# Second graph attention: where the VectorE passes over a score tile read and write

## The chip, the cores and the metric

The kernel runs on one core of one Trainium2 chip. The metric is the device time in microseconds of one execution; the figures given for a kernel are the median and the lowest and highest of its runs. TensorE is called PE here, VectorE DVE, ScalarE ACT, GpSimd POOL and SyncE SP, as in the profile.

## The reference

The program is two graph attentions over 12,500 nodes and 200,000 edges sorted by target node, each followed by a residual and a layer norm. The change touches the second one alone:

```python
src = concatenate([edge_index[0], loops]); dst = concatenate([edge_index[1], loops])
xp = (x @ W).reshape(n, H, C)                       # 12500 x 4 heads x 64
a_src = einsum('nhc,hc->nh', xp, att_src)
a_dst = einsum('nhc,hc->nh', xp, att_dst)
alpha = leaky_relu(a_src[src] + a_dst[dst], negative_slope=0.2)
amax = segment_max(alpha, dst)
ex = exp(alpha - amax[dst])
w = ex / segment_sum(ex, dst)[dst]
agg = segment_sum(xp[src] * w[..., None], dst)
out = elu(agg.reshape(n, H * C) + bias)
```

The result is added to x and normed. The self loops (`loops`) are handled by the kernel apart, block by block.

## The kernel before

The stage is `attend_plain`; its tiles' names begin with `plain_` in the trace. The edges are cut into 521 tiles of 384 (`MAIN`), each with 32 spill-over slots taken from the next tile, so that a tile has 416 slots (`SLOTS`) on the free axis. The 128 partitions are 4 heads by 32 target nodes (`TN`).

For tile t the engines do this, each in its own queue:

- POOL (`gather`, L1286) issues three indirect DMAs of 128 rows each from `xp` into `rows`, a ring of 8 tiles. Before tile t it waits only for `agg_done` of tile t-8, the tile that last used the slot.
- SP (`fetch`, L1307) loads `a_dst`, one value per partition, into a ring of 4, and puts results away (`put_out`, L1326, for tile t-7, stands just ahead of it). It also loads masks and indices.
- PE (`score`, L1378) transposes the source scores of the gathered rows into PSUM `p_s` (two buffers), [128 x 416].
- ACT (`move`, L1540) adds `a_dst` as a bias and copies `p_s` to SBUF `alpha`. ACT (`set_apart`, L1531) makes `far` in bf16: zero where slot and target node belong together and immense elsewhere.
- DVE (`lower_bound`) subtracts `far` from `alpha` and takes the maximum along the row (L1424, a fused pass and a read of its accumulator into `raw`), applies the leaky factor to the maximum (L1428, one column) and to the whole tile (L1429, 416 columns), and makes two one-column values from the maximum (L1433 `LOW`, L1434 `KEEP`). Both L1424 and L1429 read two SBUF operands of full width.
- ACT (`weigh`, L1548) takes the exponential. PE (`turn_weights`, L1363, L1364) transposes the weights into PSUM `p_w`, DVE (`copy_weights`, L1417) copies them to SBUF, PE (`aggregate`, L1391) sums the messages in `p_o` with 16 matmuls, and ACT (`put`, L1556, L1559) copies them out.

Once for each of 98 blocks of 128 nodes, DVE, ACT and SP also join the sums, add the self loop, and norm (`join`, `weigh_parts`, `gather_parts`, `finish`, `end_norm`): L1440, L1473, L1479, L1483 and L1486 are DVE passes of 256 or 264 columns with two SBUF operands.

The order in each queue is written out: `interleave` walks the steps n, and a `TilePart(lag, fn)` does tile n - lag in step n. On DVE step n holds `copy_weights` of tile n-3, `lower_bound` of tile n-1, then block work. On ACT it holds `move` of n-1, `set_apart` of n, `put` of n-4, block work, `weigh` of n-1. On PE it holds `turn_weights` of n-3, `score` of n-1, `aggregate` of n-4. Sixteen steps have three blocks' work among them. The first attention, `attend_typed`, is built alike, but its DVE pass L989 reads the scores straight from PSUM, `typed_p_s`, and its gathers are L765.

Of the kernel before, what the change touches and what calls it, by code (L numbers as in the profile page):

```python
# [10 lines left out]
ALU = mybir.AluOpType  # L11
ACT = mybir.ActivationFunctionType
AX = mybir.AxisListType.X

P = 128
# [19 lines left out]
SLOTS = MAIN + SPILL  # L35
# [1174 lines left out]
def attend_plain(k):  # L1210
# [3 lines left out]
    R, M, SCORE, TURN_LAG, LAG = 8, 4, 1, 3, 4  # L1214
    LOADS = 16
    FIRST = 73
    HALF = PERIOD // 2
    A_SRC, A_DST = VW, VW + P
    with Stage(nc, "plain") as z:
# [3 lines left out]
        far = z.sb("far", [P, 2, SLOTS], BF16)  # L1223
        a_dst = z.sb("a_dst", [P, M, 1])
        alpha = z.sb("alpha", [P, 2, SLOTS])
        raw = z.sb("raw", [P, 2])
        weight = z.sb("weight", [P, 2, SLOTS])
        weight_t = z.sb("weight_t", [P, 2, 4 * P])
        col = z.sb("col", [P, 4, 3])
        MAXED, LOW, KEEP = range(3)  # L1230
        result = z.sb("result", [P, 4, AG])
        one = z.sb("one", [P, 1])
        agg = z.sb("agg", [P, 2, HEADS * AG])
# [23 lines left out]
        p_s = z.ps("p_s", [P, 2, 512])  # L1257
# [1 line left out]
        p_o = z.ps("p_o", [P, 2, 512])  # L1259
        rows_in, match_in, index_in, result_out, slab_in = z.sems("rows_in", R), z.sems("match_in", M), z.sems("index_in", 4), z.sems("result_out", 4), z.sems("slab_in", 2)  # L1260
        own_in, out_ = z.sems("own_in", GROUP), z.sems("out", GROUP)
        (settled, slot_free, setup, init_done, far_ready, scores_ready, max_ready, low_ready, raw_ready, moved, alpha_ready, exp_done, turned,
         weight_t_ready, agg_done, result_ready, later_in) = (z.sem(n) for n in (
            "settled", "slot_free", "setup", "init_done", "far_ready", "scores_ready", "max_ready", "low_ready", "raw_ready", "moved", "alpha_ready",
            "exp_done", "turned", "weight_t_ready", "agg_done", "result_ready", "later_in"))
        settled4, keep_ready = z.sem("settled4"), z.sem("keep_ready")
        (agg_in, joined, self_added, self_ready, empty_ready, top_ready, peak_ready, below_ready, scaled_ready, weighed, total_ready, whole_ready,
# [24 lines left out]
        @block.sync  # L1292
        def _(sp):
            places = [sp.alloc_register(f"sp_place{j}") for j in range(TPB)]
            put_places = [sp.alloc_register(f"sp_put1_{j}") for j in range(TPB)]

            def fetch_index(g, at):
                sp.dma_start(index[:, g], k.idx[:, at]).then_inc(index_in[g], 16)

            def fetch(t):  # L1300
                m = t.slot(M)
                node = first_nodes(k, sp, t, places)
                if not t.known_below(M):
                    sp.wait_ge(moved, t.n - M + 1)
                    sp.sem_inc(slot_free, 1)
                with nc.allow_non_contiguous_dma(reason="one value per node and head"):
                    sp.dma_start(a_dst[:, m], k.xp[bass.ds(node, TN), A_DST:V1].rearrange("n (h o) -> h n o", o=1)).then_inc(match_in[m], 16)  # L1307
                if t.slot(TPB) == 2 and not (isinstance(t.q, int) and t.n + 2 >= TILES):
                    g, group = group_of(t)
                    if not t.known_below(TPB):  # L1310
                        sp.wait_ge(far_ready, t.n - 2)
                        sp.sem_inc(slot_free, 1)
                    fetch_slab((g + 1) % 2, bass.ds(t.n + 2, TPB))
                if t.slot(TPB) == TPB - 1:
                    g, group = group_of(t)
                    fetch_index((g + EARLY) % 4, bass.ds((group + EARLY) * CALLS, CALLS))

            def fetch_slab(slot, at):
                sp.dma_start(match[:, slot], k.match[1, at].unsqueeze(0).broadcast_to((P, TPB, SLOTS))).then_inc(slab_in[slot], 16)

            def put_out(t):
                m = t.slot(4)
                node = first_nodes(k, sp, t, put_places)
                sp.wait_ge(result_ready, t.n + 1)
                sp.sem_inc(slot_free, 1)
                sp.dma_start(k.agg[t.slot(2), bass.ds(node, TN)].rearrange("n h c -> h n c"), result[:, m]).then_inc(result_out[m], 16)  # L1326

            def load(b):
                o = b.slot(GROUP)
                if not b.known_below(GROUP):  # L1330
                    sp.wait_ge(self_done, b.n - GROUP + 1)
                sp.dma_start(own[:, o], k.xp[bass.ds(b.n * P, P), :]).then_inc(own_in[o], 16)
                sums_settled(sp, b, result_out, slot_free)
                if not b.known_below(1):
                    sp.wait_ge(joined, b.n)
                sp.dma_start(agg[:], k.agg[:, bass.ds(b.n * P, P)].rearrange("a n h c -> n a (h c)")).then_inc(agg_in, 16)

            def store(b):
                o = b.slot(GROUP)
                sp.wait_ge(res_ready, b.n + 1)  # L1340
                sp.dma_start(k.out[bass.ds(b.n * P, P), :], res[:, o]).then_inc(out_[o], 16)

            for g in range(EARLY):
                fetch_index(g, slice(g * CALLS, g * CALLS + CALLS))
            fetch_slab(0, slice(0, TPB))
            sp.wait_ge(setup, 1)
            interleave(sp, FIRST, TilePart(7, put_out), TilePart(0, fetch), BlockPart(1, 3, store), BlockPart(0, 0, load))
            for j in range(4):
                sp.wait_ge(result_out[j], 16 * -(-(TILES - j) // 4))
            groups = TILES // TPB + EARLY  # L1350
            for g in range(4):
                sp.wait_ge(index_in[g], 16 * -(-(groups - g) // 4))
            for o in range(GROUP):
                sp.wait_ge(out_[o], 16 * -(-(ROWS - o) // GROUP))

        @block.tensor
        def _(pe):
# [8 lines left out]
            def score(t):  # L1366
                c, r = t.slot(2), t.slot(R)
                if not t.known_below(2):
                    pe.wait_ge(moved, t.n - 1)
                pe.wait_ge(rows_in[r], t.use(R) * (16 * CH) + 16 * CH)  # L1370
                for j in range(CH + 1):
                    e = P if j < CH else SPILL
# [39 lines left out]
        def _(v):  # L1412
            def copy_weights(t):
# [2 lines left out]
                    v.wait_ge(agg_done, t.n - 1)  # L1416
                v.tensor_copy(weight_t[:, t.slot(2)], p_w[:, t.slot(2)]).then_inc(weight_t_ready, 1)  # L1417

            def lower_bound(t):
                c, m = t.slot(2), t.slot(4)  # L1420
                v.wait_ge(moved, t.n + 1)
                v.wait_ge(far_ready, t.n + 1)
                v.sem_inc(settled4, 1)
                v.tensor_tensor_reduce(alpha[:, c], alpha[:, c], far[:, c], 1.0, -3.0e38, ALU.subtract, ALU.max,  # L1424
                                       accum_out=raw[:, c:c + 1]).then_inc(raw_ready, 1)
                v.wait_ge(raw_ready, t.n + 1)
                maxed = col[:, m, MAXED:MAXED + 1]
                v.scalar_tensor_tensor(maxed, raw[:, c:c + 1], 0.2, raw[:, c:c + 1], ALU.mult, ALU.max).then_inc(max_ready, 1)  # L1428
                v.scalar_tensor_tensor(alpha[:, c], alpha[:, c], 0.2, alpha[:, c], ALU.mult, ALU.max).then_inc(alpha_ready, 1)  # L1429
                v.wait_ge(max_ready, t.n + 1)  # L1430
                if not t.known_below(4):
                    v.wait_ge(result_ready, t.n - 3)
                v.tensor_scalar(col[:, m, LOW:LOW + 1], maxed, NOEDGE, -1.0, ALU.max, ALU.mult).then_inc(low_ready, 1)  # L1433
                v.scalar_tensor_tensor(col[:, m, KEEP:KEEP + 1], maxed, NOEDGE, maxed, ALU.is_gt, ALU.mult).then_inc(keep_ready, 1)  # L1434

# [78 lines left out]
            for to in (p_w, result):  # L1514
# [1 line left out]
            init(v.memset(one[:], 1.0))  # L1516
            v.wait_ge(init_done, count)
            v.sem_inc(setup, 1)
            interleave(v, FIRST, TilePart(TURN_LAG, copy_weights), TilePart(SCORE, lower_bound),
                       BlockPart(2, 0, join), BlockPart(3, 1, gather_parts), BlockPart(4, 0, weigh_parts),  # L1520
                       BlockPart(5, 1, finish), BlockPart(6, 1, end_norm))

# [1 line left out]
        def _(act):  # L1524
# [6 lines left out]
                act.activation(far[:, t.slot(2)], match[:, slab, t.slot(TPB)], ACT.Square, bias=cst[:, C_CODE:C_CODE + 1],  # L1531
                               scale=FAR).then_inc(far_ready, 1)

            def move(t):
                c, m = t.slot(2), t.slot(M)
                act.wait_ge(match_in[m], t.use(M) * LOADS + LOADS)
                act.wait_ge(scores_ready, t.n + 1)
                if not t.known_below(2):
                    act.wait_ge(exp_done, t.n - 1)
                act.activation(alpha[:, c], p_s[:, c, 0:SLOTS], ACT.Identity, bias=a_dst[:, m]).then_inc(moved, 1)  # L1540

            def weigh(t):
                c = t.slot(2)
                if not t.known_below(2):
                    act.wait_ge(turned, t.n - 1)
                act.wait_ge(low_ready, t.n + 1)
                act.wait_ge(alpha_ready, t.n + 1)
                act.activation(weight[:, c], alpha[:, c], ACT.Exp, bias=col[:, t.slot(4), LOW:LOW + 1]).then_inc(exp_done, 1)  # L1548

            def put(t):  # L1550
# [26 lines left out]
            def grow(b):  # L1577
                act.wait_ge(h_ready, b.n + 1)
                if not b.known_below(1):
                    act.wait_ge(y_ready, b.n)  # L1580
                act.activation(grown[:], h[:], ACT.Exp, bias=one[:, 0:1]).then_inc(grown_ready, 1)

            act.wait_ge(setup, 1)
            interleave(act, FIRST, TilePart(SCORE, move), TilePart(0, set_apart), TilePart(LAG, put),
                       BlockPart(3, 0, scale), BlockPart(4, 1, grow), BlockPart(5, 0, own_parts), TilePart(SCORE, weigh))


# [1343 lines left out]
```

## Time and profile before

| | us |
|---|---|
| median of 3 runs | 4631.05 |
| lowest, highest | 4630.45, 4632.06 |
| span of the profiled execution | 4627.2 |
| gathers of the first attention | 350.6 to 2454.5 |
| gathers of the second attention | 2533.2 to 4569.1 |
| from the last gather to the end | 58.1 |

The page gives PE 85% of the span, DVE 74%, POOL 68% and ACT 60%. These are means over stages that have different limits, so the stage of the second attention is read by itself. A POOL instruction of kind DMA_INDIRECT is the issue of one gather, and its duration is the time POOL was occupied with issuing, not the time of the transfer. An idle time "<-issue" is one in which the engine waited for nothing that the profile shows.

### The profile page before, as it was taken

What the parts mean: (1) busy time and instruction counts of PE and PEld (TensorE: products, weight loads), DVE (VectorE), ACT (ScalarE), POOL (GpSimd) and SP (SyncE); (2) the same over time, 40 slices, a digit from 0 to 9 for tenths busy, and PEclk for the clock granted to TensorE, in tenths of its full rate; (3) what the DMA queues carried; (4) which work ended last, traced back from release to release, by engine and by line L of the source; (5) the groups of instructions that cost most, each with busy time, mean ns of one, the idle gap of its engine ahead of it and who ended that gap; (6) DMA issues with size and microseconds to landing.
All of it is one profiled execution on the core that took longest, in us unless ns stands there. A gap on an engine that the chain in (4) does not pass through costs nothing. (4 is left out here: it accounts for less than half of the span.)

```text
span 4627.2 us, 149696 instructions
## 1 busy us (share of the span) xinstructions
PE 3929.3 (85%) x42462; PEld 2568.6 (56%) x42462; DVE 3415.2 (74%) x11602; ACT 2795.2 (60%) x7985; POOL 3143.2 (68%) x3229
## 2 busy tenths in 40 slices
PE   6988999999999999999996778778877877777874
PEld 4655555555555555555554556555555555555553
DVE  3235788777777778777775578888778778787777
ACT  2324555555555555555553677777777777777775
POOL 1217777777777777777772777777777777777773
PEclk9998999999999999999997677777778777787777
DMA  6878888888888888888884777777777777777774
GB/s 207 282 236 246 259 259 259 257 259 259 259 255 260 258 260 258 257 258 261 259 256 120 187 206 206 207 204 205 207 207 205 205 204 205 205 208 209 203 206 131
DMA packets 820558, 1052.06 MB, mean 227 GB/s; under 512 B 458633, under 2 KB 632338, under 8 KB 820464
## 3 DMA queue, kind: packets, MB, share of 16 engines
q0 software_dynamic: 225072, 726.83, 53.9%
q1 hardware_dynamic: 594078, 323.35, 27.0%
q10 hardware_dynamic: 1314, 0.99, 0.1%
q14 instruction: 80, 0.66, 0.0%
q8 instruction: 14, 0.23, 0.0%
HBM read 915.79 MB, written 133.39 MB: 227 GB/s over the span
## 5 line engine op out<-in xcount | busy, mean ns | idle before, releaser
L1286 POOL DMA_INDIRECT plain_rows<-xp,plain_index x1563 | 1559.8, 998 | 554.9 <-issue 440.8
L765 POOL DMA_INDIRECT typed_rows<-kv,typed_index x1563 | 1511.2, 967 | 626.2 <-issue 414.3
L1391 PE MATMUL plain_p_o<-plain_rows,plain_weight_t 128*64 128x130 f32 (+1 forms) x8336 | 856.5, 348 | 44.0 <-DVE plain_weight_t L1417 43.3
L1158 ACT ACTIVATE typed_weight<-typed_weight,typed_col 128x416 f32<-128x416 f32 x521 | 334.6, 642 | 855.0 <-DVE typed_col L991 809.5
L1378 PE MATMUL plain_p_s<-all_cst,plain_rows 128*128 128x128 f32 (+1 forms) x2084 | 455.0, 318 | 368.2 <-DMA plain_rows<-xp,plain_index 365.9
L1391 PEld LDWEIGHTS plain_p_o<-plain_rows,plain_weight_t 128*64 128x64 f32 (+1 forms) x8336 | 570.2, 169 | 203.8 <-issue 128.5
L1378 PEld LDWEIGHTS plain_p_s<-all_cst,plain_rows 128*128 128x128 f32 (+1 forms) x2084 | 335.2, 174 | 522.6 <-issue 504.8
L989 DVE CUSTOM_DVE_ANT_0 typed_weight<-typed_p_s,typed_far 128x416 f32<-128x416 f32 x521 | 305.1, 586 | 371.5 <-PE typed_p_s L874 347.8
L874 PE MATMUL typed_p_s<-typed_kt,typed_q 64*32 64x416 f32 x4168 | 472.4, 521 | 103.4 <-issue 73.0
L1424 DVE CUSTOM_DVE_ANT_0 plain_alpha<-plain_alpha,plain_far 128x416 f32<-128x416 f32 x521 | 310.0, 595 | 311.4 <-ACT plain_alpha L1540 296.4
L962 DVE TENSOR_TENSOR typed_kt<-typed_p_kt,typed_rel 128x768 f32<-128x768 f32 x521 | 494.7, 950 | 3.7 <-PE typed_p_kt L851 3.4
L1548 ACT ACTIVATE plain_weight<-plain_alpha,plain_col 128x416 f32<-128x416 f32 x521 | 331.4, 636 | 256.2 <-DVE plain_col L1433 250.4
L851 PE MATMUL typed_p_kt<-all_cst,typed_rows 128*128 128x128 f32 x3126 | 458.4, 283 | 6.8 <-DMA typed_rows<-kv,typed_index 6.3
L1559 ACT COPY plain_result<-plain_p_o 32x65 f32<-32x65 f32 x2084 | 425.4, 204 | 18.2
L889 PE MATMUL typed_p_o<-typed_rows,typed_weight_t 128*32 128x65 f32 (+1 forms) x16672 | 413.4, 225 | 3.0 <-ACT typed_result L1165 0.4
L1363 PE MATMUL plain_p_w<-all_cst,plain_weight 128*128 128x128 f32 x1563 | 360.5, 351 | 50.0 <-ACT plain_weight L1548 48.9
L851 PEld LDWEIGHTS typed_p_kt<-all_cst,typed_rows 128*128 128x128 f32 x3126 | 334.6, 142 | 98.2 <-issue 90.6
L1540 ACT ACTIVATE plain_alpha<-plain_p_s,plain_a_dst 128x416 f32<-128x416 f32 x521 | 316.7, 608 | 119.9 <-PE plain_p_s L1378 95.7
L1417 DVE COPY plain_weight_t<-plain_p_w 128x512 f32<-128x512 f32 x521 | 355.3, 682 | 32.1 <-PE plain_p_w L1364 20.5
L889 PEld LDWEIGHTS typed_p_o<-typed_rows,typed_weight_t 128*32 128x32 f32 (+1 forms) x16672 | 279.6, 108 | 168.2 <-issue 91.1
L1531 ACT ACTIVATE plain_far<-plain_match,all_cst 128x416 bf16<-128x416 uint8 x521 | 328.6, 631 | 9.0 <-DMA plain_match<-match 9.0
L1138 ACT ACTIVATE typed_far<-typed_match,all_cst 128x416 bf16<-128x416 uint8 x521 | 334.0, 641 | 0.0
(190 smaller groups left out, 6303.5 us busy)
## 6 DMA issues: line engine op xcount, KB each, us to landing
typed_match<-match SPq DMA_DIRECT2D x131, 208.0 KB
plain_match<-match SPq DMA_DIRECT2D x131, 208.0 KB
agg<-qkv_zero SPq DMA_DIRECT2D x98, 264.0 KB
typed_agg<-agg SPq DMA_DIRECT2D x98, 264.0 KB
plain_agg<-agg SPq DMA_DIRECT2D x98, 264.0 KB
kv<-qkv_kv SPq DMA_DIRECT2D x98, 258.0 KB
typed_kinds<-match SPq DMA_DIRECT2D x131, 192.0 KB
typed_rows<-kv,typed_index POOLq DMA_INDIRECT x1563
```

The lines of the kernel that those rows point to most:

```text
L765: pool.indirect_dma_start(rows[:, r, j, :], None, k.kv, bass.IndirectOffsetOnAxis(ap=index[:, g, at:at + 1], axis=0)).then_inc(rows_in[r], 16)
L851: last = pe.transpose(p_kt[:, pair, j * P:j * P + P], rows[:, t.slot(R), j, pair * P:pair * P + P], ident)
L874: last = pe.matmul(p_s[at:at + TN, 0:SLOTS], q[own, m, :, h // 2], kt[own, h // 2, lo:lo + SLOTS], start=True, stop=True, tile_position=(H ...
L889: last = pe.matmul(p_o[at:at + TN, 0:V], weight_t[0:e, t.slot(2), j * P + at:j * P + at + TN], v[:, D + V * h:D + V * h + V], start=j == 0 ...
L962: v.tensor_tensor(kt[:, :, lo:lo + MAIN], p_kt[:, :, 0:MAIN], both_pairs(0, MAIN), ALU.add).then_inc(kt_ready, 1)
L1158: act.activation(weight[:, c], weight[:, c], ACT.Exp, bias=col[:, t.slot(4), LOW:LOW + 1]).then_inc(exp_done, 1)
L1286: pool.indirect_dma_start(rows[:, r, j, :], None, k.xp, bass.IndirectOffsetOnAxis(ap=index[:, g, at:at + 1], axis=0)).then_inc(rows_in[r], 16)
L1363: pe.transpose(p_w[:, t.slot(2), j * P:j * P + P], weight[:, t.slot(2), j * P:j * P + P], ident)
L1378: last = pe.transpose(p_s[:, c, j * P:j * P + e], a_src[:, A_SRC:A_DST], ident[0:e, 0:e])
L1391: last = pe.matmul(p_o[at:at + HC, t.slot(2), 0:2 * V], weight_t[0:e, t.slot(2), j * P + at:j * P + at + HC], val[:, 2 * V * g:2 * V * g + ...
L1417: v.tensor_copy(weight_t[:, t.slot(2)], p_w[:, t.slot(2)]).then_inc(weight_t_ready, 1)
L1559: last = act.copy(result[at:at + TN, m, 0:V], p_o[at:at + TN, t.slot(2), V * (h % 2):V * (h % 2) + V])
```

## The change

The leaky ReLU is made from two branches. ACT (`dampen`) writes 0.2 * score + 0.2 * a_dst into a new SBUF tile `damped`, instead of score + a_dst into `alpha`. It needs 0.2 * a_dst, which a new one-column DVE step `dampen_target` makes for tile n in step n. DVE then computes max(score + a_dst, damped) in place in PSUM `p_s`, and the pass with the maximum reads `p_s` and `far` and writes `alpha`. The maximum now is already that of the leaky scores, so L1428 and L1429 are gone. `p_s` is given back to PE at `raw_ready` instead of `moved`, and the slot of `a_dst` to SP at `leaked`.

```diff
@@ fetch (SP)
-                    sp.wait_ge(moved, t.n - M + 1)
+                    sp.wait_ge(leaked, t.n - M + 1)
@@ score (PE)
-                    pe.wait_ge(moved, t.n - 1)
+                    pe.wait_ge(raw_ready, t.n - 1)
@@ (DVE)
+            def dampen_target(t):
+                m = t.slot(M)
+                v.wait_ge(match_in[m], t.use(M) * LOADS + LOADS)
+                if not t.known_below(M):
+                    v.wait_ge(damped_ready, t.n - M + 1)
+                v.tensor_scalar(a_fifth[:, m], a_dst[:, m], 0.2, None, ALU.mult).then_inc(fifth_ready, 1)
+
             def lower_bound(t):
                 c, m = t.slot(2), t.slot(4)
-                v.wait_ge(moved, t.n + 1)
+                v.wait_ge(damped_ready, t.n + 1)
+                v.scalar_tensor_tensor(p_s[:, c, 0:SLOTS], p_s[:, c, 0:SLOTS], a_dst[:, m], damped[:, c], ALU.add, ALU.max).then_inc(leaked, 1)
                 v.wait_ge(far_ready, t.n + 1)
+                v.wait_ge(leaked, t.n + 1)
+                if not t.known_below(2):
+                    v.wait_ge(exp_done, t.n - 1)
                 v.sem_inc(settled4, 1)
-                v.tensor_tensor_reduce(alpha[:, c], alpha[:, c], far[:, c], 1.0, -3.0e38, ALU.subtract, ALU.max,
+                v.tensor_tensor_reduce(alpha[:, c], p_s[:, c, 0:SLOTS], far[:, c], 1.0, -3.0e38, ALU.subtract, ALU.max,
                                        accum_out=raw[:, c:c + 1]).then_inc(raw_ready, 1)
                 v.wait_ge(raw_ready, t.n + 1)
-                maxed = col[:, m, MAXED:MAXED + 1]
-                v.scalar_tensor_tensor(maxed, raw[:, c:c + 1], 0.2, raw[:, c:c + 1], ALU.mult, ALU.max).then_inc(max_ready, 1)
-                v.scalar_tensor_tensor(alpha[:, c], alpha[:, c], 0.2, alpha[:, c], ALU.mult, ALU.max).then_inc(alpha_ready, 1)
-                v.wait_ge(max_ready, t.n + 1)
...
+                maxed = raw[:, c:c + 1]
@@
-            interleave(v, FIRST, TilePart(TURN_LAG, copy_weights), TilePart(SCORE, lower_bound),
+            interleave(v, FIRST, TilePart(TURN_LAG, copy_weights), TilePart(SCORE, lower_bound), TilePart(0, dampen_target),
@@ (ACT)
-            def move(t):
+            def dampen(t):
                 c, m = t.slot(2), t.slot(M)
-                act.wait_ge(match_in[m], t.use(M) * LOADS + LOADS)
+                act.wait_ge(fifth_ready, t.n + 1)
                 act.wait_ge(scores_ready, t.n + 1)
                 if not t.known_below(2):
-                    act.wait_ge(exp_done, t.n - 1)
-                act.activation(alpha[:, c], p_s[:, c, 0:SLOTS], ACT.Identity, bias=a_dst[:, m]).then_inc(moved, 1)
+                    act.wait_ge(leaked, t.n - 1)
+                act.activation(damped[:, c], p_s[:, c, 0:SLOTS], ACT.Identity, bias=a_fifth[:, m], scale=0.2).then_inc(damped_ready, 1)
@@ weigh (ACT)
-                act.wait_ge(alpha_ready, t.n + 1)
```

On DVE, one step of the loop of `attend_plain` before (ISA is the fused pass with its maximum and the read of the accumulator; REGISTER_ALU is the sequencer's):

```order
L1417 COPY plain_weight_t<-plain_p_w 128x512
L1421 REGISTER_ALU
L1424 ISA plain_alpha,plain_raw<-plain_alpha,plain_far 128x416
L1424 ISA plain_raw 128x1
L1428 SCALAR_TENSOR_TENSOR plain_col<-plain_raw 128x1
L1429 SCALAR_TENSOR_TENSOR plain_alpha<-plain_alpha 128x416
L1433 TENSOR_SCALAR plain_col<-plain_col 128x1
```

And the same step of DVE's queue in the changed kernel, with its own line numbers:

```order
L1419 COPY plain_weight_t<-plain_p_w 128x512
L1430 REGISTER_ALU
L1431 SCALAR_TENSOR_TENSOR plain_p_s<-plain_p_s,plain_a_dst,plain_damped 128x416
L1437 ISA plain_alpha,plain_raw<-plain_p_s,plain_far 128x416
L1437 ISA plain_raw 128x1
L1443 TENSOR_SCALAR plain_col<-plain_raw 128x1
L1444 SCALAR_TENSOR_TENSOR plain_col<-plain_raw 128x1
```

The full-width leaky pass moved from behind the maximum to ahead of it. The one-column L1428 is gone, and L1426 (`plain_a_fifth<-plain_a_dst`) stands behind L1444 in every step, ahead of the block work. On ACT the order is the same in both kernels; its first pass of a step has another output and bias.

## Rows read from the trace of the kernel before

**Rows 1.** The page's first line.
```profile
span 4627.2 us, 149696 instructions
```

**Rows 2.** Stages by window: start:end, us, busy us and instructions per engine, clock, DMA.
```profile
core 0: us, PE busy (x) PEld busy (x) DVE busy (x) ACT busy (x) POOL busy (x), PEclk, DMA share, GB/s
350.60:2454.50 2103.90, 1990.89 (x28122) 1193.42 (x28121) 1623.71 (x4550) 1139.36 (x2835) 1511.21 (x1563) 0.99 0.89 258
...
2533.20:4569.10 2035.90, 1587.38 (x12396) 1147.83 (x12396) 1592.30 (x6404) 1507.38 (x4689) 1559.76 (x1563) 0.76 0.78 205
```

**Rows 3.** POOL's groups: busy us, mean ns | idle before and releasers; durations min/median/max.
```profile
L1286 POOL DMA_INDIRECT plain_rows<-xp,plain_index x1563 | 1559.8, 998 | 554.9 <-issue 440.8 <-DMA plain_index<-all_idx 78.7 <-PE plain_p_o L1391 35.4
L765 POOL DMA_INDIRECT typed_rows<-kv,typed_index x1563 | 1511.2, 967 | 626.2 <-issue 414.3 <-PE typed_p_o L889 178.3 <-DVEq L1125 33.6
...
L1286 POOL DMA_INDIRECT plain_rows<-xp,plain_index x1563: 942/949/1372, 2533.2 to 4568.1; - x196
```

**Rows 4.** Timeline, second attention: gathers that start inside a DVE pass (start, us).
```profile
3814.34 0.58 DVE L1429 SCALAR_TENSOR_TENSOR plain_alpha<-plain_alpha 128x416 f32<-128x416 f32 x1
3814.40 1.35 POOL L1286 DMA_INDIRECT plain_rows<-xp,plain_index  x1 [0.30 <-issue]
...
4094.78 0.59 DVE L1424 CUSTOM_DVE_ANT_0 plain_alpha<-plain_alpha,plain_far 128x416 f32<-128x416 f32 x1 [0.28 <-ACT plain_alpha L1540]
4094.95 1.24 POOL L1286 DMA_INDIRECT plain_rows<-xp,plain_index  x1 [0.30 <-PE plain_p_o L1391]
...
2964.34 0.42 DVE L1479 TENSOR_TENSOR plain_h<-plain_part,plain_self_part 128x256 f32<-128x256 f32 x1
2964.39 1.19 POOL L1286 DMA_INDIRECT plain_rows<-xp,plain_index  x1 [0.30 <-issue]
...
3800.02 0.67 DVE L1417 COPY plain_weight_t<-plain_p_w 128x512 f32<-128x512 f32 x1
3800.27 0.94 POOL L1286 DMA_INDIRECT plain_rows<-xp,plain_index  x1 [0.30 <-PE plain_p_o L1391]
```

**Rows 5.** Timeline, first attention: a gather that starts inside the pass L989.
```profile
375.76 0.59 DVE L989 CUSTOM_DVE_ANT_0 typed_weight<-typed_p_s,typed_far 128x416 f32<-128x416 f32 x1 [1.24 <-PE typed_p_s L874]
375.83 0.95 POOL L765 DMA_INDIRECT typed_rows<-kv,typed_index  x1 [0.30 <-issue]
```

**Rows 6.** DVE's groups by form, whole span.
```profile
L989 DVE CUSTOM_DVE_ANT_0 typed_weight<-typed_p_s,typed_far 128x416 f32<-128x416 f32 x521 | 305.1, 586 | 371.5 <-PE typed_p_s L874 347.8 <-DVE typed_rstd L348 11.8 <-issue 10.3
L1424 DVE CUSTOM_DVE_ANT_0 plain_alpha<-plain_alpha,plain_far 128x416 f32<-128x416 f32 x521 | 310.0, 595 | 311.4 <-ACT plain_alpha L1540 296.4 <-issue 7.1
L1429 DVE SCALAR_TENSOR_TENSOR plain_alpha<-plain_alpha 128x416 f32<-128x416 f32 x521 | 307.4, 590 | 0.0
L1433 DVE TENSOR_SCALAR plain_col<-plain_col 128x1 f32<-128x1 f32 x521 | 75.4, 145 | 0.0
L1479 DVE TENSOR_TENSOR plain_h<-plain_part,plain_self_part 128x256 f32<-128x256 f32 x98 | 41.7, 425 | 3.4
L1417 DVE COPY plain_weight_t<-plain_p_w 128x512 f32<-128x512 f32 x521 | 355.3, 682 | 32.1 <-PE plain_p_w L1364 20.5 <-issue 9.3 <-PE plain_p_o L1391 0.4
L1515 DVE MEMSET plain_p_w<- 128x1024 f32 x1 | 0.9, 912 | 11.4 <-PEq L232 11.4
```

**Rows 7.** DVE's own timeline around one tile, with ACT's L1548 behind it.
```profile
3500.49 0.59 DVE L1424 CUSTOM_DVE_ANT_0 plain_alpha<-plain_alpha,plain_far 128x416 f32<-128x416 f32 x1 [0.91 <-ACT plain_alpha L1540]
...
3501.01 0.08 DVE L1424 DVE_READ_ACCUMULATOR2_ANT plain_raw<- 128x1 f32 x1
3501.13 0.16 DVE L1428 SCALAR_TENSOR_TENSOR plain_col<-plain_raw 128x1 f32<-128x1 f32 x1
...
3501.70 0.14 DVE L1433 TENSOR_SCALAR plain_col<-plain_col 128x1 f32<-128x1 f32 x1
```

**Rows 8.** Waits from 2700 to 4400 us: us in total, times, longest.
```profile
DVE plain_alpha L1424 <- ACT plain_alpha L1540: 216.1, 275, 2.9
...
DVE plain_weight_t L1417 <- PE plain_p_w L1364: 9.9, 17, 0.9
```

**Rows 9.** SP's queue in the timeline: a result put away, then the next `a_dst` issued.
```profile
3501.88 0.61 SPq L1326 DMA_DIRECT2D agg<-plain_result  x1
...
3503.70 0.61 SPq L1307 DMA_DIRECT2D plain_a_dst<-xp  x1
```

More of the change, by code:

```diff
@@ L1225, in attend_plain @@
         alpha = z.sb("alpha", [P, 2, SLOTS])
+        a_fifth = z.sb("a_fifth", [P, M, 1])
+        damped = z.sb("damped", [P, 2, SLOTS])
         raw = z.sb("raw", [P, 2])
@@ L1228, in attend_plain @@
         weight_t = z.sb("weight_t", [P, 2, 4 * P])
-        col = z.sb("col", [P, 4, 3])
-        MAXED, LOW, KEEP = range(3)
+        col = z.sb("col", [P, 4, 2])
+        LOW, KEEP = range(2)
         result = z.sb("result", [P, 4, AG])
@@ L1261, in attend_plain @@
         own_in, out_ = z.sems("own_in", GROUP), z.sems("out", GROUP)
-        (settled, slot_free, setup, init_done, far_ready, scores_ready, max_ready, low_ready, raw_ready, moved, alpha_ready, exp_done, turned,
+        (settled, slot_free, setup, init_done, far_ready, scores_ready, low_ready, raw_ready, leaked, damped_ready, fifth_ready, exp_done, turned,
          weight_t_ready, agg_done, result_ready, later_in) = (z.sem(n) for n in (
-            "settled", "slot_free", "setup", "init_done", "far_ready", "scores_ready", "max_ready", "low_ready", "raw_ready", "moved", "alpha_ready",
+            "settled", "slot_free", "setup", "init_done", "far_ready", "scores_ready", "low_ready", "raw_ready", "leaked", "damped_ready", "fifth_ready",
             "exp_done", "turned", "weight_t_ready", "agg_done", "result_ready", "later_in"))
@@ L1583, in _ @@
             act.wait_ge(setup, 1)
-            interleave(act, FIRST, TilePart(SCORE, move), TilePart(0, set_apart), TilePart(LAG, put),
+            interleave(act, FIRST, TilePart(SCORE, dampen), TilePart(0, set_apart), TilePart(LAG, put),
                        BlockPart(3, 0, scale), BlockPart(4, 1, grow), BlockPart(5, 0, own_parts), TilePart(SCORE, weigh))
```

## The prediction

> **What bounds the kernel now.** I read the stages first. The second attention issues its gathers from 2533.2 to 4569.1 us, a stretch of 2035.9 us in a span of 4627.2 [rows 1, 2]. In it POOL is busy 1559.8 us, DVE 1592.3, PE 1587.4 and ACT 1507.4 [rows 2]. Busy time does not pick one of them, so I went to what each waits for. POOL waits for nobody. Of its 554.9 us of idle time, 78.7 lie before its first gather, and the rest is the gap of 0.30 us in front of every gather. Where the row names PE as the releaser, the gap is the same 0.30 [rows 3, 4], so that wait was over before the gap was. POOL therefore issues back to back, 1563 times, with a period of 2035.9 / 1563 = 1.303 us. DVE, between 2700 and 4400 us, stands 226 us waiting for ACT and PE [rows 8]; in those 1700 us there are 1700 / 3.908 = 435 tiles (a tile is three gathers, 3.908 us), so DVE has 0.52 us of slack per tile. The bound of the stage is POOL's issuing, and every 0.01 us on a gather is 15.6 us of the kernel.
>
> The gather's own duration is where the profile speaks. Its median is 949 ns, its mean 998, its maximum 1372 [rows 3]. Something lengthens some gathers by up to 0.4 us. The timeline says what. A gather that starts 0.06 us into L1429 lasts 1.35 us, one 0.17 us into L1424 lasts 1.24, one 0.05 us into the shorter L1479 lasts 1.19. One 0.25 us into L1417, which reads PSUM and is longer than all of these, lasts 0.94 [rows 4]. The excess over 0.95 fits one rule: the time from the gather's start to the end of the DVE pass, less 0.12 to 0.13. First case: pass ends at 3814.92, gather starts at 3814.40, 0.52 left, excess 0.40. Second: 0.42 left, excess 0.29. Third: 0.37 left, excess 0.24. The gather stands still, from 0.12 us after its start until the DVE pass is over, if that pass reads two SBUF operands. In the first attention the same fused pass reads its scores from PSUM, and only `far` from SBUF. A gather that starts 0.07 us into it lasts 0.95 [rows 5]. That is nearly the change in miniature, already on the chip.
>
> **Part 1, the stalls of the gathers.** All excess in the stage is 1559.8 - 1563 x 0.949 = 76.5 us. The change takes it away where it comes from L1424 and L1429, and leaves it for the five block passes. To split it, let gathers start at random: a pass of length L costs (L - 0.13)^2 / (2 x 1.303) us. For 0.59 us that is 0.081 us, times 1042 passes 84.6; for 0.42 us (L1479's row, the four others taken alike) it is 0.032, times 490 passes 15.8 [rows 6]. The sum of 100.4 is over the 76.5 measured, since starts are not random, so both are scaled by 0.76: 64.5 us for the tile passes, 12.0 for the blocks. Bounds: at best all 76.5 go. At worst the blocks keep as much as the whole excess of the first attention, which has no such tile pass, 1511.2 - 1563 x 0.949 = 28 us [rows 3], and 48.5 go. I take 64.5, the value worked out from this stage's own rows.
>
> The Trainium skill weighs in here, in "SBUF — State Buffer", section "Who interferes with whom". It says that a VectorE instruction with two SBUF inputs contends with a GpSimd instruction that reads SBUF, through a shared read interface. The row on L1429 agrees. The same passage infers that writing descriptors needs only the write side, and that tensor_tensor did not stall such a DMA; by that the term would be 0 instead of 64.5, and it is rival C.
>
> **Part 2, DVE per tile.** Removed: L1428, 0.16 us, of which 0.07 to 0.12 shows on the queue, and L1429, 0.590. Added: a pass in PSUM of 416 columns, and `dampen_target`, one column, 0.145 like L1433 [rows 6]. The fused pass now reads PSUM, like L989, 586 against 595: nothing [rows 6]. From the start of L1424 to the end of L1433 it is 3501.84 - 3500.49 = 1.35 us now [rows 7]. Afterwards: 0.59, a hop of 0.04 (accumulator read ends 3501.09, L1428 starts 3501.13), 0.60 from L1424's start to the end of that read, 0.04, 0.14: 1.41. With `dampen_target` behind it DVE has some 0.15 us more per tile, and POOL gives it 64.5 / 521 = 0.12 us less time. Of 0.52 slack 0.25 remains, so DVE hides it. The value that no row shows is the price of a pass that reads and writes the same PSUM tile. The lower bound is L1429's 0.590; writing alone into PSUM costs 0.912 / 1024 = 0.89 ns a column [rows 6], no more than a column of L1417 takes. The upper bound is that read and write take turns, one more column time for each column: 416 x 0.912 / 1024 = 0.37, so 0.96 us. I take 0.59, because L1417's and L989's reads and the memset's write are each at full pace and nothing in the rows shows the two sides disturbing one another.
>
> **Part 3, waits that move.** On PE, `score` of tile t waits for `raw_ready` of t-2 instead of `moved`. In the same step `turn_weights` of t-2 stands ahead and waits for its exponential, which is later still; cost 0. On SP, `a_dst` of tile t is now asked for when `leaked` of t-4 has come, some 0.6 us later than `moved`, and it is needed by DVE at the end of step t instead of by ACT in step t+1. In the rows SP puts away tile t-7, whose copy ACT makes in step t-3, at 3501.88, and issues `a_dst` of t at 3503.70 [rows 9]. The end of step t lies three steps of 3.9 us behind, near 3513, and 9 us are more than enough for half a kilobyte. Behind this wait DVE would have all its block work queued, and ACT would wait for `fifth_ready`; while the lead is 9 us the cover holds. ACT keeps its passes; `dampen` comes after `weigh` of the tile before, and `dampen_target` ends about 0.25 us after `LOW`, well inside the 0.64 us of the exponential. The gathered traffic comes faster by 3%: the DMA share would go from 0.78 to 0.81, under the 0.89 that the first attention sustains [rows 2]. The tail of 58 us behind the last gather and the other stages are untouched.
>
> **Sum.** 4627.2 - 64.5 = 4562.7 for the profiled span; the median lies 3.9 above that span now, so 4566.
>
> **Rivals.** A: the change only does half of what it says. The new pass reads `damped` and the scalar `a_dst` from SBUF, two SBUF sources though one is a single column, and no row has such a form next to a gather. If it still holds POOL, only the half of L1424 goes: 32 us, 4599. Against it: a column of one element is read once and not all along the pass.
>
> B, slower: DVE becomes the bound. The point is 0.52 us more work per tile: then DVE's queue takes 3.91 us a tile, as POOL does now. With the upper price of the PSUM pass it has 0.15 + 0.37 = 0.52, exactly there, and then waits on ACT between passes no longer fit under POOL's pace. If a quarter of today's waiting, 0.13 us, stays, it is 521 x 0.13 = 68 us on top of today: 4699. The ring of 8 would fill and POOL's gaps before a gather would grow beyond 0.30.
>
> C: the excess is not a matter of two SBUF operands, and the gathers go on being stalled as often: POOL's time is unchanged, 4631. Against it stand L1417's and L989's rows [rows 4, 5].
>
> D: the stalls go, but DVE's remaining 0.25 us are a mean over steps with and without block work. With three blocks in 16 steps DVE falls behind for some, and POOL then waits for `agg_done`. If a third of the gain goes back, 4588. The buffers speak against it: no gap of POOL is now over 0.30.
>
> **How the numbers follow.** Forecast 0.70, A 0.08, D 0.10, C 0.04, B 0.08. The forecast has its own bounds, 4554.5 (all excess gone) to 4582.5 (48.5 gone). A range of 4551 to 4606 takes in the forecast, A and D with a few us for the split, and leaves B and C out, 0.12. What a measurement of this kernel can tell from no change is 0.2%, 9 us. Faster 0.87: forecast, A, D, less a little. Same 0.05: C and some of D. Slower 0.08: B.
>
> **What would show it.** The gathers' mean should fall to 0.949 + 12 / 1563 = 0.957 us, their last end to about 4505, with the gap in front still 0.30. Long gathers should start in block passes only. The PSUM pass should last 0.59 us, and DVE's waits for ACT should shrink by about half. Right in time but wrong in reason would be a gather mean still near 0.998 with something else shorter. The prediction is wrong if the PSUM pass takes over 0.9 us, if gathers that start in it last 1.2 to 1.35, or if POOL's idle time before gathers grows beyond 0.30 each.

## The result, and the profile after

| | before | after |
|---|---|---|
| median, us | 4631.55 (4 runs) | 4712.8 (4 runs, 4710.2 to 4717.3) |
| ratio | 1 | 1.0179, interval 1.0167 to 1.0192 |
| span of the profiled execution | 4627.2 | 4708.8 |
| gathers of the second attention, us | 2035.9 | 2111.4 |

The changed kernel is 1.8% slower, 81 us, where 65 us less were forecast. The page's first line, its row on POOL's gathers, and the rows of the two DVE passes of full width in the view by form (columns as in [rows 3, 6]):

```profile
span 4708.8 us, 150898 instructions
...
L1288 POOL DMA_INDIRECT plain_rows<-xp,plain_index x1563 | 1488.4, 952 | 702.8 <-issue 443.5
...
L1431 DVE SCALAR_TENSOR_TENSOR plain_p_s<-plain_p_s,plain_a_dst,plain_damped 128x416 f32<-128x416 f32 x521 | 340.2, 653 | 104.0 <-ACT plain_damped L1550 101.4 <-issue 2.3
L1437 DVE CUSTOM_DVE_ANT_0 plain_alpha<-plain_p_s,plain_far 128x416 f32<-128x416 f32 x521 | 308.4, 592 | 93.7 <-DVE plain_p_s L1431 55.2 <-issue 38.5
```

The gathers did what was forecast. Their mean is 952 ns after 998 [rows 3], and POOL is busy 71.4 us less. A gather that starts 0.10 us into the new leaky pass is not held (timeline: start, then duration, to be read against [rows 4]):

```profile
3504.75 0.65 DVE L1431 SCALAR_TENSOR_TENSOR plain_p_s<-plain_p_s,plain_a_dst,plain_damped 128x416 f32<-128x416 f32 x1
3504.85 0.94 POOL L1288 DMA_INDIRECT plain_rows<-xp,plain_index  x1 [0.30 <-issue]
```

It is so throughout the trace: 384 gathers start in one of the two new passes with 0.15 us or more of it left, and none lasts over 0.96 us; in the kernel before, 397 start so in L1424 or L1429, and they last up to 1.37. Those over 1.1 us went from 242 to 39.

But POOL now waits. The gathers' stretch by window (columns as in [rows 2]) and POOL's waits in the second attention:

```profile
2535.70:4647.10 2111.40, 1616.57 (x12376) 1166.33 (x12376) 1663.92 (x6390) 1495.88 (x4678) 1488.35 (x1563) 0.74 0.75 198
```

```profile
POOL plain_rows L1288 <- PE plain_p_o L1393: 179.6, 168, 3.5
```

The stretch holds 2111.4 - 1488.4 = 623 us without a gather, where it was 476; +147 and -71 are the +75 of the stretch. The wait named is the one for a free slot in the ring of 8 (`agg_done`). Its longest is 3.5 us, where a gap before a gather was 0.30 [rows 4]. The slot is freed by PE, and PE in turn waits for DVE's copy of the weights. PE's wait from 2700 to 4400 us (us in total, times, longest), first in the kernel before and then in the changed one:

```profile
PE plain_p_o L1391 <- DVE plain_weight_t L1417: 36.7, 35, 2.8
```

```profile
PE plain_p_o L1393 <- DVE plain_weight_t L1419: 260.1, 114, 5.3
```

DVE's own waits in the same window, to be read against [rows 8]:

```profile
DVE plain_weight_t L1419 <- issue: 113.2, 24, 5.6
DVE plain_p_s L1431 <- ACT plain_damped L1550: 51.2, 80, 0.8
DVE plain_alpha L1437 <- DVE plain_p_s L1431: 42.4, 237, 0.2
DVE plain_alpha L1437 <- issue: 32.6, 180, 0.5
```

The first line is new. The same line of the kernel before reads:

```profile
DVE plain_weight_t L1417 <- issue: 8.8, 20, 0.5
```

DVE stands still 24 times for 4.7 us, on the mean, with nothing that the profile names as a releaser, in front of `copy_weights`. In the timeline these places are one turn of the loop apart (16 steps, some 66 us), and each is the first instruction behind the loop's branch:

```profile
3473.07 0.18 DVE L1474 RECIPROCAL plain_total<-plain_total 128x4 f32<-128x4 f32 x1
...
3477.48 0.69 DVE L1419 COPY plain_weight_t<-plain_p_w 128x512 f32<-128x512 f32 x1 [4.03 <-issue]
```

And on the page, the DMA queue that carries instructions (packets, MB, share), first of the kernel before and then of the changed one:

```profile
q14 instruction: 80, 0.66, 0.0%
```

```profile
q14 instruction: 216, 1.77, 0.1%
```

136 packets more, five in each of 27 turns, 1.1 MB or 41 KB a turn. Of all queues only this one moved noticeably more. The loop of DVE in the second attention has 337 instructions in the kernel before, waits and register operations counted, and 374 in the changed one. The branch's own record begins at 3473.37 and the next record of DVE's sequencer 3.91 us later; before, that interval is 0.32 to 0.34 us.

The trace's list of DMA packets has the times of this queue's packets as well. In the kernel before, none of its packets of 8192 bytes moves while the loop turns (first branch at 2889 us, last at 4516). In the changed kernel five move in each turn. At the branch shown, one starts at 3475.33 and ends at 3475.67, and DVE goes on at 3477.28. It is so in all 27 turns: a packet starts within the pause, 2.8 us behind the branch, and DVE goes on 1.56 us after that packet's end (medians; the second is never under 1.06 nor over 1.65).

### The profile page after: what moved, and what is told of

It is laid out like the page before. It is cut to its first block and busy times, and to the rows that moved or that the text cites. A ratio compares the mean times of both kernels' runs of the same rounds, so it can differ in the third digit from the quotient of the medians.

```text
span 4708.8 us, 150898 instructions
## 1 busy us (share of the span) xinstructions
PE 3962.3 (84%) x42462; PEld 2589.6 (55%) x42462; DVE 3491.1 (74%) x11602; ACT 2787.4 (59%) x7985; POOL 3071.8 (65%) x3229
## 5 line engine op out<-in xcount | busy, mean ns | idle before, releaser
L1288 POOL DMA_INDIRECT plain_rows<-xp,plain_index x1563 | 1488.4, 952 | 702.8 <-issue 443.5
L1393 PE MATMUL plain_p_o<-plain_rows,plain_weight_t 128*64 128x130 f32 (+1 forms) x8336 | 883.3, 356 | 304.0 <-DVE plain_weight_t L1419 303.9
L1393 PEld LDWEIGHTS plain_p_o<-plain_rows,plain_weight_t 128*64 128x64 f32 (+1 forms) x8336 | 588.3, 173 | 472.5 <-DVE plain_weight_t L1419 319.7
L989 DVE CUSTOM_DVE_ANT_0 typed_weight<-typed_p_s,typed_far 128x416 f32<-128x416 f32 x521 | 305.3, 586 | 371.6 <-PE typed_p_s L874 347.6
L1380 PE MATMUL plain_p_s<-all_cst,plain_rows 128*128 128x128 f32 (+1 forms) x2084 | 441.0, 319 | 46.4 <-DMA plain_rows<-xp,plain_index 46.2
L1431 DVE SCALAR_TENSOR_TENSOR plain_p_s<-plain_p_s,plain_a_dst,plain_damped 128x416 f32<-128x416 f32 x521 | 340.2, 653 | 104.0 <-ACT plain_damped L1550 101.4
L1437 DVE CUSTOM_DVE_ANT_0 plain_alpha<-plain_p_s,plain_far 128x416 f32<-128x416 f32 x521 | 308.4, 592 | 93.7 <-DVE plain_p_s L1431 55.2
L1365 PEld LDWEIGHTS plain_p_w<-all_cst,plain_weight 128*128 128x128 f32 x1563 | 204.2, 171 | 303.8 <-ACT plain_weight L1557 188.2
L1550 ACT ACTIVATE plain_damped<-plain_p_s,plain_a_fifth 128x416 f32<-128x416 f32 x521 | 316.6, 608 | 42.0 <-PE plain_p_s L1380 20.8
```

The lines of the kernel that those rows point to most:

```text
L1288: pool.indirect_dma_start(rows[:, r, j, :], None, k.xp, bass.IndirectOffsetOnAxis(ap=index[:, g, at:at + 1], axis=0)).then_inc(rows_in[r], 16)
L1365: pe.transpose(p_w[:, t.slot(2), j * P:j * P + P], weight[:, t.slot(2), j * P:j * P + P], ident)
L1380: last = pe.transpose(p_s[:, c, j * P:j * P + e], a_src[:, A_SRC:A_DST], ident[0:e, 0:e])
L1393: last = pe.matmul(p_o[at:at + HC, t.slot(2), 0:2 * V], weight_t[0:e, t.slot(2), j * P + at:j * P + at + HC], val[:, 2 * V * g:2 * V * g + ...
L1431: v.scalar_tensor_tensor(p_s[:, c, 0:SLOTS], p_s[:, c, 0:SLOTS], a_dst[:, m], damped[:, c], ALU.add, ALU.max).then_inc(leaked, 1)
```

## The experiments

Two theories to begin with. **F**: the stall behind the branch is a reload of instructions, it costs 27 x 4.3 = 116 us of DVE's time and is the cause. **W**: DVE's passes and waits per tile have become longer, and that is the cause. From e5 on, **L** is F in the form that the loop's length alone decides, and its rival **P** says that the stall belongs to the changed kernel's passes or waits. "Inert" waits are waits on a semaphore that is already full; two in a row become one instruction. In all edits below the loop is DVE's in `attend_plain`. "Gap" is the time from the record of the loop's branch to DVE's next record, as the median over the turns. A ratio is to the kernel before, run beside each experiment.

**e1: the same loop, elsewhere.** The changed kernel with inert waits ahead of the loop.

```diff
+            for _ in range(240):
+                v.wait_ge(init_done, count)
             interleave(v, FIRST, TilePart(TURN_LAG, copy_weights), ...
```

> The changed kernel with 240 waits on a semaphore that is already full (120 instructions) put ahead of DVE's loop of the second attention, so that the loop starts 120 instructions later; nothing in the loop changes. Theory F (the branch at the loop's end stalls DVE some 4.3 us in each of 27 turns because of where the 374 instructions of the loop lie, in lines of 256): the gap behind the branch falls from about 4.6 us to 0.3, 27 x 4.3 = 116 us of DVE's time come back, and the time is 4580 to 4620. Theory W (DVE is the bound only by the longer passes and waits of each tile, the gap is a wait for something else): the gap and the time stay, 4700 to 4715.

Measured: 4719.98 us, ratio 1.0204 (1.0187 to 1.0221), gap 4.7 us in 27 turns. The expectation of F by place missed: with the loop 120 instructions further on, the stall is the same. That rules out a rule in lines of 256 instructions, for which one of two places 120 apart would do, but not every rule of place, as is worked out below. This kernel alone does not tell whether the stall is the cause of the lost time.

**e2: the loop of before in the place of the stalling one.**

```diff
+            for _ in range(280):
+                v.wait_ge(init_done, count)
             interleave(v, FIRST, TilePart(TURN_LAG, copy_weights), ...
```

> The kernel before with 280 such waits (140 instructions) ahead of the same loop, so that its 337 instructions start at the same place as the stalling loop of the changed kernel. Theory F by place: a gap of 4 to 5 us behind the branch in each of 27 turns. Since DVE has 0.52 us of slack per tile, 8.3 us per turn of 16 tiles, most of it is absorbed: 4631 to 4690. Theory F by length alone (374 instructions are too many wherever they lie, 337 are not): gap 0.3 us, 4631. Theory W: 4631.

Measured: 4630.51 us, ratio 1.0006 (0.9996 to 1.0015), gap 0.30 us. Counted in the program's order, DVE's loop begins with instruction 2907 in both this kernel and the changed one. From that place a loop of 337 instructions does not stall, and one of 374 does.

**e3: a shorter loop.** The changed kernel without two waits per tile that others imply: the exponential of tile t-2 is over when its weights have been turned, for which `copy_weights` waited earlier in the same step, and `damped_ready` has been waited for in the step itself.

```diff
                 v.wait_ge(leaked, t.n + 1)
-                if not t.known_below(2):
-                    v.wait_ge(exp_done, t.n - 1)
@@ dampen_target
-                if not t.known_below(M):
-                    v.wait_ge(damped_ready, t.n - M + 1)
```

> The changed kernel without two waits per tile that other waits already imply (exp_done ahead of the pass with the maximum, damped_ready in dampen_target): 342 instructions in DVE's loop instead of 374, starting one instruction later than in the kernel before. Theory F: the stall behind the branch is gone, 4570 to 4610. Theory W: the waits cost 0.02 to 0.05 us each, 521 x 0.04 to 0.1 = 20 to 50 us, 4660 to 4695, with the gap behind the branch still there.

Measured: 4570.63 us, ratio 0.9872 (0.9856 to 0.9889). 342 instructions, gap 0.33 us. The page's queue of instructions, and the stretch of the gathers by window:

```profile
q14 instruction: 80, 0.66, 0.0%
```

```profile
2537.20:4511.90 1974.70, 1556.34 (x12359) 1122.38 (x12359) 1649.25 (x6391) 1493.56 (x4679) 1486.91 (x1563) 0.77 0.79 211
```

The stall and the 136 packets are gone, and the kernel is 142 us faster than the changed one. Repeated as **e11**, beside e10 on another chip:

> e3_trim once more, on the chip and in the rounds of e10: 4570 within 5 us, the yardstick for e10.

4573.37 us, ratio 0.9875 (0.9859 to 0.9891).

**e6 and e9: the short loop made longer again, with nothing.** e3 plus inert waits, in every step (358 instructions) and in every second one (350).

```diff
+            def inert(t):
+                for _ in range(2):
+                    v.wait_ge(init_done, 3)
...
-  TilePart(0, dampen_target),
+  TilePart(0, dampen_target), TilePart(0, inert),
```

In e9 the range is `2 if t.c % 2 else 0`.

> e3_trim with two waits on a full semaphore per step, one instruction each tile: 358 instructions in DVE's loop instead of 342. Theory L leaves open on which side this falls: if over the limit, gap 4 to 5 us and 4680 to 4712; if under it, gap 0.3 and e3's 4570.6 plus 521 x 0.03 to 0.05 us, 4575 to 4600. Rival P: 4575 to 4600.

> e3_trim with two waits on a full semaphore in every second step: 350 instructions in DVE's loop, half way between 342 (no stall) and 358 (stall). No theory names the side. If the limit is over 350: gap 0.3 us and 4570 to 4585. If under: gap 4.5 us and 4695 to 4715.

Measured: e6 4707.4 us, ratio 1.0167 (1.0150 to 1.0184), gap 4.5 us. e9 4699.6 us, 1.0149 (1.0129 to 1.0168), gap 4.6 us. e9's eight instructions that do nothing, in a loop of 342, cost some 130 us. With the stall back by them alone, most of the 142 us between e3 and the changed kernel is the stall's; some 14 us (1.0149 against 1.0179) are left for the waits that e3 left out. The same steps stand unrolled ahead of the loop too, so e9's loop also begins 36 instructions further on than e3's, and e6's 73. e9's queue of instructions:

```profile
q14 instruction: 216, 1.76, 0.1%
```

**e5: the stall in the kernel before.** Five inert waits in each step, 377 instructions; every pass as it was.

```diff
+                for _ in range(5):
+                    v.wait_ge(init_done, 3)
```

> The kernel before with five waits on a full semaphore at the end of every step in DVE's queue: 377 instructions in the loop instead of 337, all passes as they were. Theory L (a loop body above some length between 342 and 374 instructions makes DVE stand 4 to 5 us behind its branch in every turn, whatever the instructions are): gap 4 to 5 us in 27 turns. DVE had 0.52 us of slack per tile, 8.3 per turn; the inert waits take 0.1 to 0.15 per tile, 2 per turn, and the stall 4.4: the time is 4631 to 4680, so the stall is there and mostly free. Rival P (the stall belongs to the new passes or waits of the changed kernel): gap 0.3 us, 4631.

Measured: 4639.95 us, ratio 1.0020 (1.0010 to 1.0029), gap 4.6 us in 27 turns. DVE's waits from 2700 to 4400 us and the queue of instructions:

```profile
DVE plain_alpha L1424 <- ACT plain_alpha L1544: 127.3, 211, 2.1
DVE plain_weight_t L1417 <- issue: 112.3, 23, 6.3
```

```profile
q14 instruction: 215, 1.76, 0.1%
```

Rival P falls: the stall needs none of the changed kernel's passes. And it is nearly free there. 112 us of stall stand in the place of 89 us in which DVE waited for ACT [rows 8: 216.1, here 127.3], and the kernel loses 11 us, the 40 inert instructions a turn included. The same stall costs 130 us once the slack of DVE has been spent.

**e4: where the new pass's price comes from.** e1 with the leaky pass writing to SBUF. That version of the loop still has 374 instructions, so it stalls; the rows of its passes are what it tells. The wait for `exp_done` moves ahead of the leaky pass, which now is the first to write `alpha`.

```diff
-                v.scalar_tensor_tensor(p_s[:, c, 0:SLOTS], p_s[:, c, 0:SLOTS], a_dst[:, m], damped[:, c], ALU.add, ALU.max).then_inc(leaked, 1)
+                v.scalar_tensor_tensor(alpha[:, c], p_s[:, c, 0:SLOTS], a_dst[:, m], damped[:, c], ALU.add, ALU.max).then_inc(leaked, 1)
...
-                v.tensor_tensor_reduce(alpha[:, c], p_s[:, c, 0:SLOTS], far[:, c], 1.0, ...
+                v.tensor_tensor_reduce(alpha[:, c], alpha[:, c], far[:, c], 1.0, ...
```

> As e1_pad120, but the leaky pass writes its result to SBUF alpha instead of back into PSUM, and the pass with the maximum reads alpha and far, both in SBUF. If the write to PSUM is what made the leaky pass 653 ns instead of 590 and the hop behind it 0.18 us instead of 0.04, the pass falls to about 590 and the hop to 0.05, which gives DVE 0.19 us a tile back; if it is the PSUM read beside an SBUF read, 653 stays. Gathers that start in the pass with the maximum are held again, mean about 975 ns instead of 952: 30 to 40 us. By theory F in all 4590 to 4630, near e1; by theory W (DVE's work per tile is the bound) 4712 - 521 x 0.19 = 4613 with the gap behind the branch still there.

Measured: 4715.73 us, ratio 1.0192 (1.0175 to 1.0209).

```profile
L1433 DVE SCALAR_TENSOR_TENSOR plain_alpha<-plain_p_s,plain_a_dst,plain_damped 128x416 f32<-128x416 f32 x521 | 335.9, 645 | 101.0 <-ACT plain_damped L1552 95.2 <-issue 2.6 <-ACT plain_weight L1559 1.6
```

The pass lasts 645 ns with an SBUF output and 653 with a PSUM output. Writing back into PSUM costs 8 ns, the other 55 over the old 590 come with the inputs (PSUM beside SBUF where both were in SBUF, and a column as the scalar for a constant; which of them was not tried). The hop of 0.18 us behind it stays too.

**e8: half of the change.** The same edit on e3, without a stall in the way.

> e3_trim with the leaky pass writing to SBUF alpha and the maximum taken from alpha and far, both in SBUF: one of the two passes with two SBUF operands is back, nothing else. By the term of the prediction (half of 64.5 us): gathers of 970 to 975 ns instead of 951, 1563 x 0.02 = 30 us, 4590 to 4605. Rival (DVE's queue is the bound of e3, not POOL): no more than 10 us, 4570 to 4580.

Measured: 4589.35 us, ratio 0.9911 (0.9895 to 0.9928), 19 us over e3.

```profile
L1288 POOL DMA_INDIRECT plain_rows<-xp,plain_index x1563 | 1518.1, 971 | 557.5 <-issue 435.8 <-DMA plain_index<-all_idx 80.3 <-PE plain_p_o L1393 41.4
```

One pass with two SBUF operands lengthens the gathers from 951 to 971 ns, 31 us in sum, as the forecast has it for a half. Of these, 19 reach the end. POOL's idle time before its gathers, apart from the first, is 487.7 us in e3 and 477.2 here, so some 10 of the 31 fill time in which POOL of e3 waited.

**e7 and e10: the last hop.** In e7 `dampen_target` of the next tile stands between the leaky pass and the maximum. In e10 the leaky pass (`leak`) stands ahead of `copy_weights`.

```diff
@@ e7
                 v.scalar_tensor_tensor(p_s[:, c, 0:SLOTS], ...).then_inc(leaked, 1)
+                if not isinstance(t.q, int) or t.n + 1 < TILES:
+                    dampen_target(t.back(-1))
                 v.wait_ge(far_ready, t.n + 1)
@@ e10
-            interleave(v, FIRST, TilePart(TURN_LAG, copy_weights), TilePart(SCORE, lower_bound), TilePart(0, dampen_target),
+            interleave(v, FIRST, TilePart(SCORE, leak), TilePart(TURN_LAG, copy_weights), TilePart(SCORE, lower_bound), TilePart(0, dampen_target),
```

> e3_trim with dampen_target put between the leaky pass and the pass with the maximum, where DVE stands 0.18 us waiting for its own result. Theory: the one-column step fills that hop, DVE is 0.08 to 0.15 us per tile shorter, its queue no longer holds POOL up (gap in front of a gather always 0.30), and the time falls to the bound of the gathers: 2537 + 1563 x 1.251 + 58 = 4551, so 4550 to 4562. Rival: the one-column step does not fit in the hop since the fused pass waits from its end again; the time stays at 4565 to 4575.

> e3_trim with the leaky pass put ahead of copy_weights in DVE's step, so that the 0.68 us copy stands where DVE waits 0.18 us for its own result. Theory (0.18 us from the end of a pass to the start of one that reads its result, whatever stands between): 0.13 us per tile come back to DVE, 2 us in a turn, POOL is held up less, 4550 to 4565. Rival (the order now makes the copy wait for ACT's damped scores, and the later weights hold PE and the ring of rows): 4575 to 4620.

Measured: e7 4574.39 us, ratio 0.9881 (0.9865 to 0.9898), no better than e3; from the leaky pass's end to the next pass it is still 0.18 us. e10 4615.94 us, ratio 0.9968 (0.9955 to 0.9980), worse than e11, which ran beside it, by 43 us. In both, the theory missed and the rival's range held. e10's DVE groups, and DVE's waits from 2700 to 4400 us:

```profile
L1429 DVE SCALAR_TENSOR_TENSOR plain_p_s<-plain_p_s,plain_a_dst,plain_damped 128x416 f32<-128x416 f32 x521 | 342.3, 657 | 294.4 <-ACT plain_damped L1549 287.4 <-issue 6.9
...
L1436 DVE CUSTOM_DVE_ANT_0 plain_alpha<-plain_p_s,plain_far 128x416 f32<-128x416 f32 x521 | 302.7, 581 | 0.3 <-DVE plain_p_s L1429 0.3
```

```profile
DVE plain_p_s L1429 <- ACT plain_damped L1549: 209.6, 297, 1.5
```

The hop is gone (0.3 us of idle time in all ahead of L1436, where the changed kernel has 93.7). But the copy of 0.68 us now lies inside the circle in which ACT's damped scores, DVE's two passes and ACT's exponential wait for each other, and DVE waits 209.6 us for ACT, where it waits 60.0 in e3 and 61.2 in e11. A filled hop is worth nothing if the filler lengthens the circle.

## Why the prediction was wrong

**The bound before, and the stalls of the gathers: right.** POOL was the bound, and a DVE pass with two SBUF operands held its gathers. POOL's busy time fell by 71.4 us, where 64.5 were summed and 76.5 were the limit; the mean is 952 ns against a forecast of 957. With half of the change (e8) 31 us of it are still there. The rule quoted from the Trainium skill, that a pass with two SBUF inputs contends with a GpSimd instruction that reads SBUF, agrees with these rows: the fall from 998 to 952 came with no other change to what POOL does. Its inference would spare a gather such a stall, and the gathers were stalled. A gather also reads its indices from SBUF, though, so no run here tells whether that read was held or the writing of descriptors.

**The waits that move (part 3): right as far as the rows show.** SP's `a_dst` held nobody up, and no wait of PE on `raw_ready` shows.

**The step that failed is part 2, DVE per tile**, in two ways.

First, it counted passes and the hops between them, and no instructions. The change adds a step, `dampen_target`, and several waits to each of the 16 steps of the loop: 37 instructions in all, a price the sum puts at nothing. Eight loops were tried: 337 at two places and 342 at one, all without the stall; 350, 358, 374 at two places and 377 with it. It is shown that waits that do nothing turn the stall on, and that the queue of instructions then moves 1.76 MB instead of 0.66. It is shown too that DVE's restart follows a packet of that queue: in the changed kernel, e1, e4, e5, e6 and e9, in all 27 turns, DVE goes on 1.5 to 1.6 us (medians) after the end of a packet that started within the pause, and in the loops without the stall no such packet moves. So the stall is a wait for instructions; what the packet holds is not in the trace.

What is not shown is that the length alone decides. In the stalling loops, the packets away from the branch start 119 to 132 of DVE's instructions apart, so an 8192-byte packet stands for about 128 instructions. Against such a step, e1's move by 120 and e2's by 140 shift the loop by only 8 and 12 instructions. An estimate: lay borders every 128 instructions in the program's order, at 64 and so on. Then the loops that do not stall (begin 2767, 2768 and 2907) touch three of the cells between borders, and so does the one of 280 in the first attention (1187). All that stall (begin 2804, 2841, 2907, 2944 and 3027) touch four. Borders at 59 to 72 do as well. By this reading a loop of 350 could go free at a better place, and one of 300 could stall at a worse. No run moved a loop by some 50 instructions, which would settle it.

The Trainium skill, in "Runtime: NRT & Kernel Launch", section "Instruction fetch mechanics", says that most engines hold 32 KiB of instructions in two blocks of 256, and that a taken branch to a target outside them waits for a DMA. The wait for a packet behind the branch agrees. By two blocks of 256 alone, a loop of 374 would fit at one at least of two places 120 apart, and it stalled at both, so the two blocks are not the whole rule. The page would have been reason enough to count.

Second, what it did count was too small. The leaky pass was taken at 0.59 us and is 0.65 (between the bounds of 0.59 and 0.96, at the low end). The hop from it to the pass that reads its result was taken at 0.04 us, from the hop behind an accumulator read, and is 0.18. From the start of the first pass to the end of `LOW` it is 1.62 us (median over the tiles), where 1.41 was worked out. With `dampen_target` behind it, the time from the start of the first pass to the block work went from 1.34 us to some 1.67 (medians, the latter in e3): 0.33 us more a tile, where 0.15 was summed. DVE's slack of 0.52 us a tile therefore fell by 0.12 + 0.33 to some 0.07, not to 0.25; in e3 DVE still waits 60.0 us for ACT in 1700, 0.13 us a tile. Either way there was no room for the stall: 4.3 us a turn are 0.27 us a tile.

The two together are the result; e5 and e3 separate them. The stall on the old slack costs 11 us (e5). The longer passes without the stall (e3) give 4570.6, within 5 us of the forecast's 4566, with the gathers' stretch at 1974.7 where 2035.9 - 64.5 = 1971.4 was forecast. That closeness is partly luck: in e3 POOL is busy 72.9 us less, not 64.5, and idle between gathers 11.5 us more, not 0. Both the longer passes and the stall cost 81 where a gain of 65 was due.

**The rivals.** B had the right side and nearly the right time (4699), and its point, 0.52 us of DVE's work per tile, was the right quantity. Its mechanism, a PSUM pass of 0.96 us, was not what happened: 8 ns is what the write costs (e4), and that its time came close is luck. Of the prediction's signs of being wrong, the one on POOL's idle time showed, and those on the PSUM pass and on gathers that start in it did not. A and C fall with the gathers' mean. D, block work of DVE that now reaches POOL, may be the 11.5 us of idle time in e3; that they come from block work was not shown.

**The version to keep** is e3: the change with two waits per tile less, 4570.6 us, 1.3% under the kernel before and 3% under the change as it was made.

## What to carry to other kernels

Before adding instructions to a loop, count the whole body on that engine, waits and register operations included, and compare it with the longest body that is known to run without a pause; here eight inert instructions cost 130 us. Where the body begins may count as well, so measure the pause behind the branch again after any edit ahead of the loop. Spend slack in one account: a stall that an engine with 0.5 us of slack per tile hides to within 0.2% becomes the bound once a good change elsewhere has used the slack up. When an engine is idle "for issue" in front of the same instruction once per turn, look at the branch and at the queue of instructions before looking at semaphores.

## What was not expected of the hardware

- A loop of 350 instructions or more on DVE paused for 4.5 to 4.8 us (medians) behind its branch in all 27 turns, one of 342 or fewer for 0.30 to 0.33 us. Moving the loop by 120 (at 374) or 140 instructions (at 337) changed nothing, but both are near the 128 or so that one packet of the instruction queue stands for; whether place counts beside length stays open. In the changed kernel PE, ACT, SP and POOL showed no such pause.
- In such a pause a packet of the instruction queue arrives, and DVE's next instruction comes 1.5 to 1.6 us (medians) after that packet's end.
- From the end of a full DVE pass to the start of the next that reads its result, 0.18 us pass, whether the result lies in PSUM or in SBUF (e4). A one-column step put in between did not shorten it (e7); with a copy of 0.68 us in between, no idle time was left (e10).
- An in-place pass over 416 columns of PSUM lasts 653 ns, and 645 with an SBUF output.
